# Attention and mixture-of-experts kernel: each head of a pair on its own 64 rows of the array for scores, transposed scores and halved mask matmuls

## The reference, cut to what matters

```python
def attention(X, enc, causal_mask, padding_mask, Wq, bq, Wk, bk, Wv, bv, Wo, bo):
    # 8 batches of 256 rows; 32 query heads of width 16; 8 key/value heads, each shared by 4 query heads
    q = (X @ Wq.T + bq).reshape(b, LQ, G, HPG, HD).transpose(0, 2, 3, 1, 4)
    k = (enc @ Wk.T + bk).reshape(b, LKV, G, HD).transpose(0, 2, 1, 3)
    v = (enc @ Wv.T + bv).reshape(b, LKV, G, HD).transpose(0, 2, 1, 3)
    scores = jnp.einsum('bgrqd,bgkd->bgrqk', q, k) / jnp.sqrt(HD)
    scores = jnp.where(causal_mask, -inf, scores)
    scores = jnp.where(padding_mask, -inf, scores)
    w = softmax(scores)
    out = jnp.einsum('bgrqk,bgkd->bgrqd', w, v)
    return out.transpose(...).reshape(b, LQ, HID) @ Wo.T + bo
x = x + tanh(g_xattn) * attention(layernorm(x), ctx, ...)
x = x + tanh(g_ffn) * experts(layernorm(x))      # 2 shared experts, 8 routed experts, top 2
```

## Time and profile before

| | us |
|---|---|
| median of 3 runs (1140.6 to 1146.6) | 1146.4 |
| span of the profiled execution | 1141.4 |
| PE busy / weight loads busy | 970.7 / 734.0 |
| DVE / ACT / POOL busy | 547.2 / 377.5 / 414.4 |
| attention, up to the start of the experts' matmuls | 562 |
| mean granted PE clock | 0.933 |

### The profile page before, as it was taken

How to read it: one execution, slowest core, us unless ns; L and a number is a source line. 1 busy time by engine, 2 the same in 40 slices (tenths; PEclk the granted TensorE clock), 3 DMA queues, 4 the chain that set the end, 5 groups by cost and what they waited for, 6 DMA issues and landing times.

```text
span 1141.4 us, 19977 instructions
## 1 busy us (share of the span) xinstructions
PE 970.7 (85%) x5240; PEld 734.0 (64%) x5241; DVE 547.2 (48%) x1679; ACT 377.5 (33%) x676; POOL 414.4 (36%) x513
## 2 busy tenths in 40 slices
PE   1477999999999999796499998999699898889894
PEld 1454555555555554343399987898598787778893
DVE  5286657676667677522233356633133333333331
ACT  2112544454445454362122252222122332133320
POOL 8713323333333303025100022053435665456542
PEclk9776999999999999997699997899899999999998
DMA  4333231414141323301451331143245544653442
GB/s 175 83 87 93 62 83 44 138 44 138 43 137 43 101 60 84 119 19 55 163 199 37 115 115 39 46 70 69 67 135 137 147 99 101 151 137 62 74 83 37
DMA packets 44943, 105.31 MB, mean 92 GB/s; under 512 B 8169, under 2 KB 12873, under 8 KB 43289
## 3 DMA queue, kind: packets, MB, share of 16 engines
q1 hardware_dynamic: 33064, 82.27, 24.3%
...
...
## 4 chain that ended last, share of the span: by engine, by line
PE 49%; DMA 12%; issue 11%; POOL 8%; DVE 8%; ACT 4%; POOLq 2%; ACTq 1%; SPq 1%; DVEq 0%
PE score_bank L516 5%; PE front_bank L464 5%; PE y_bank L1188 5%; PE gate_bank L1188 5%; PE up_bank L1188 5%; PE pv_bank L552 5%; DMA out_dram<-y,add_idx 5%; PE prob_bank L536 4%; PE tail_bank L464 4%; PE prob_bank L539 4%; POOL w_lo L126 3%; DMA x_ring<-xn_buf,gather_idx 3%; POOL row_table L1112 2%; DVE score_bank L780 2%; DMA row_table<-row_now 2%
## 5 line engine op out<-in xcount | busy, mean ns | idle before, releaser
L780 DVE CUSTOM_DVE_ANT_0 score_bank<-score_bank,mask 128x256 f32<-128x256 f32 x512 | 204.6, 449 | 123.5 <-PE score_bank L516 122.4
L669 ACT ACTIVATE probs<-prob_bank 128x512 f32<-128x512 f32 x256 | 150.0, 598 | 212.0 <-PE prob_bank L539 210.3
L516 PE MATMUL score_bank<-k_stack,q_stack 128*128 128x512 f32 x256 | 135.5, 533 | 31.0 <-DVE w_raw L780 16.7
L536 PE MATMUL prob_bank<-q_stack,k_stack 128*128 128x512 f32 x256 | 109.8, 436 | 15.4 <-DMA q_stack<-w_lo 12.8
L126 POOL TENSOR_TENSOR w_lo<-w_raw,w_hi (+2 forms) x20 | 70.7, 3721 | 118.5 <-ACT w_hi L120 118.5
L516 PEld LDWEIGHTS score_bank<-k_stack,q_stack 128*128 128x128 f32 x256 | 52.3, 205 | 92.9 <-DVE w_raw L780 64.5
L1399 DVE TENSOR_TENSOR h<-up_bank,silu 128x352 f32<-128x352 f32 x71 | 37.2, 525 | 154.3 <-PE up_bank L1188 118.2
L1188 PE MATMUL gate_bank<-w_hi,xt_hi 128*128 (+2 forms) x284 | 101.3, 357 | 4.5 <-DVE xt_lo L1391 2.5
L1188 PE MATMUL up_bank<-w_hi,xt_hi 128*128 (+1 forms) x284 | 93.9, 330 | 11.2 <-POOL w_lo L126 11.2
L539 PE MATMUL prob_bank<-maskT,w_raw 128*128 128x512 bf16 x256 | 102.6, 401 | 0.0
L1319 ACT ACTIVATE xt_hi<-xt_bank 128x512 fp32r<-128x512 f32 x71 | 42.5, 598 | 181.0 <-PE xt_bank L1221 168.6
...
## 6 DMA issues: line engine op xcount, KB each, us to landing
...
```

The source lines that it names most:

```text
L516: pe.matmul(bank[:].rearrange("p a b -> p (a b)"), q_stack[m.parity][:, gp, r, c * P:(c + 1) * P], k_stack[m.parity][:, gp].rearrange("p a ...
L536: pe.matmul(bank, k_stack[n.parity][:, gp, g2, kc * P:(kc + 1) * P], q_stack[n.parity][:, gp, 2 * rp:2 * rp + 2, :].rearrange("p a b -> p ...
L669: act.activation(probs[:, v % 8, :], prob_bank[v % 2][:].rearrange("p a b -> p (a b)"), ACT.Exp, scale=HD ** -0.5).then_inc(exp_done, 1)
L780: last = dve.tensor_tensor_reduce(out=bank[:, g2, :], in0=bank[:, g2, :], in1=mask[m.parity][:, c, :], scale=1.0, scalar=-3e38, op0=ALU.ad ...
```

## The change

A pair's two heads get disjoint halves of the array's rows. Source row j of a pair now lands in rows 4j, 4j+1 and 4j+2 for the three pieces (`stacked`), and rows 4j+3 hold the aux rows, so that head 0's 16 source rows fill rows 0 to 63 and head 1's fill rows 64 to 127. `k_stack` loses its second, zero-padded copy; `parity`, `k_raw` and one of two `k_hi` and `k_lo` operations go. A unit is now one head with both halves of its 256 queries (before: both heads, one half). Units are issued in pairs, in even slots: 4 score matmuls of 64 rows and 256 columns fill both score banks; 2 transposed-score matmuls of 64 rows and 512 columns fill both prob banks; the mask matmul of each bank is cut in a lower and an upper 64-row half, one before and one after the score matmuls, with a wait on a new semaphore `half_masked` between them. The waits of a pair's both units stand before its first score matmul (`score_ready` for u and u+1). `PROB_LAG` goes from 3 to 4, each half of `stack` issues 14 DMAs instead of 13, and the maxima go out in 2 DMAs.

```diff
-AUX = 3 * PAIR
+HALF = P // 2
+PARTS_A_ROW = 4
+AUX = 3
...
-PROB_LAG = 3
-PV_LAG = PROB_LAG + 5
+PROB_LAG = 4
+PV_LAG = PROB_LAG + 4
...
-STACK_DMAS = 13
+STACK_DMAS = 14
...
+        def stacked(stack, piece):
+
+            return stack[piece:P:PARTS_A_ROW]
+
+        def aux_rows(stack, g2, first=0, n=2):
+
+            lo = HALF * g2 + AUX + PARTS_A_ROW * first
+            return stack[lo:lo + PARTS_A_ROW * (n - 1) + 1:PARTS_A_ROW]
...
-                    for part, (q, k) in enumerate([(q_hi, k_hi), (q_hi, k_lo), (q_lo, k_hi)]):
-                        dst = slice(PAIR * part, PAIR * (part + 1))
-                        copy_rows(sp, qs[dst, gp, :, :], q[src, :, :]).then_inc(stack_in[half], 16)
-                        copy_rows(sp, ks[dst, gp, :, :], k[src, :, :]).then_inc(stack_in[half], 16)
-                copy_rows(sp, qs[AUX:AUX + 4, GP // 2 * half:GP // 2 * (half + 1), :, :], zeros).then_inc(stack_in[half], 16)
+                    for piece, (q, k) in enumerate([(q_hi, k_hi), (q_hi, k_lo), (q_lo, k_hi)]):
+                        copy_rows(sp, stacked(qs, piece)[:, gp, :, :], q[src, :, :]).then_inc(stack_in[half], 16)
+                        copy_rows(sp, stacked(ks, piece)[:, gp, :], k[src, :]).then_inc(stack_in[half], 16)
+                for g2 in range(2):
+                    copy_rows(sp, aux_rows(qs, g2)[:, GP // 2 * half:GP // 2 * (half + 1)].rearrange("o g r s -> o (g r s)"),
+                              aux_rows(k_stack[0], g2, 2, 4).rearrange("o g s -> o (g s)")).then_inc(stack_in[half], 16)
...
-            def score_unit(m, u):
-                gp, r, c = u // (R * QC), u // QC % R, u % QC
+            def score_ready(m, u):
+
                 if u % (SCORE_UNITS // 2) == 0:
-
                     at_least(pe, stack_in[2 * u // SCORE_UNITS], 16 * STACK_DMAS * (m.index + 1))
-                bank = score_bank[(m.parity + u) % 2]
                 if u == 0:
                     at_least(pe, maxima_done, SCORE_UNITS * m.index)
                 elif u == 1:
                     at_least(pe, maxT_copied, m.index)
                 else:
                     at_least(pe, maxima_done, SCORE_UNITS * m.index + u - 1)
-                pe.matmul(bank[:].rearrange("p a b -> p (a b)"), q_stack[m.parity][:, gp, r, c * P:(c + 1) * P],
-                          k_stack[m.parity][:, gp].rearrange("p a b -> p (a b)"),
-                          start=True, stop=True).then_inc(scores_done, 1)
+
+            def score_half(m, u, c):
+                gp, r, g2 = u // (R * 2), u // 2 % R, u % 2
+                rows = slice(HALF * g2, HALF * (g2 + 1))
+                last = pe.matmul(score_bank[(m.parity + u) % 2][:, c, :],
+                                 q_stack[m.parity][rows, gp, r, c * P:(c + 1) * P], k_stack[m.parity][rows, gp, :],
+                                 start=True, stop=True)
+                if c == QC - 1:
+                    last.then_inc(scores_done, 1)
+
+            def score_pair(m, u):
+
+                for k in range(2):
+                    score_ready(m, u + k)
+                for c in range(QC):
+                    for k in range(2):
+                        score_half(m, u + k, c)
...
-            def prob_unit(n, v):
+            def prob_scores(n, v):
...
                 at_least(pe, exp_done, PROB_UNITS * n.index + v - 1)
...
+            low, high = slice(0, HALF), slice(HALF, P)
+
+            def unit_pairs(s, n, score, soft, pair):
+
+                u, v = 2 * pair, 2 * pair - PROB_LAG
+                score, soft = score and u < SCORE_UNITS, soft and 0 <= v < PROB_UNITS
+                if soft:
+                    for k in range(2):
+                        prob_scores(n, v + k)
+                if soft and score:
+                    prob_mask(n, v, low, False, half_masked)
+                    prob_mask(n, v + 1, high, False, half_masked)
+                if score:
+                    score_pair(s, u)
+                if soft and score:
+                    at_least(pe, half_masked, (PROB_UNITS - PROB_LAG) * n.index + v + 2)
+                    prob_mask(n, v, high, True)
+                    prob_mask(n, v + 1, low, True)
+                elif soft:
+                    for k in range(2):
+                        prob_mask(n, v + k, slice(0, P), True)
...
-                    if score and slot < SCORE_UNITS:
-                        score_unit(s, slot)
-                    if soft and 0 <= slot - PROB_LAG < PROB_UNITS:
-                        prob_unit(n, slot - PROB_LAG)
+                    if slot % 2 == 0:
+                        unit_pairs(s, n, score, soft, slot // 2)
```

70 lines of the change are left out of this document (35 added, 35 removed).

## The result

| | before | changed |
|---|---|---|
| median, us | 1145.06 (4 runs) | 1174.63 (1164.39 to 1184.58, 4 runs) |
| ratio, 95% interval | | 1.0234 (1.0178 to 1.029) |
| span of the profiled execution | 1141.4 | 1182.8 |
| PE / DVE / ACT busy | 970.7 / 547.2 / 377.5 | 976.8 / 541.6 / 364.6 |
| the experts' first matmul | 562.6 | 595.4 |

The kernel became slower, by about the predicted time (1176). The profiled execution is the longest of the four (1184.58), 1.7% above the shortest, and is left out of the ratio; 8.6 of its extra 41.4 lie behind the start of the experts' matmuls, in code that the change doesn't touch: there PE's half-clock spells come and go from run to run. What the change did is read up to that start: 595.4 - 562.6 = 32.8 more, where 32.5 were forecast.

A forecast was written before the change was run, and what follows sets the result against it. PE and DVE were taken to alternate, with paired handshakes deciding. Iteration terms of 14.5 + 3 + 4.5 + 6.5 + 4 made +32.5 on the profiled 1141.4, so 1174, stated as 1176; 8-in-10 range 1152 to 1205.

The forecast's parts named there:

- The overlap: On PE, two 64-row halves run fully at the same time: four steps cost 0.95 a pair instead of 1.4, gaining 0.46.
- The rival with weight loads in series: Handshakes bind and score weight loads run one after another: 0.19 a pair, 21 more in all, 1197; chance 0.12.
- p4 to p6: Pairs of slots 8 to 13, with query blocks, a projection and the key/value block; PE-bound, forecast 0.7 shorter, 17.3 together.
- The handshakes: Deciding term: PE waits for both units of the last pair, losing overlap with DVE and ACT; +2.9 a full iteration.
- The ACT loop: A pair's second transposed-score matmul needs both previous exponentials, these the second mask halves behind the scores: 2.49 a cycle.
- The DVE loop: PE starts a pair's scores only after DVE finished both previous units: 0.05 + 0.41 + 1.46 + 0.14 = 2.06, plus extras.
- 0.5 for `tail_hi` between the exponentials: In the pair of slots 24 and 25, this ACT work adds 0.5, making the pair 3.0.
- The sign that DVE would wait 0.4 to 0.5 for scores in every light pair: Expected profile evidence in the eleven pairs without much other PE work: DVE waits 0.4 to 0.5 for scores.
- Over the iterations: Sum over attention: 14.5 (n = 1 to 5) + 3 + 4.5 + 6.5 (n = -1) + 4 (clock) = +32.5.
- The clock: Sparsely used PE drops to half clock in p1 and p2: 0.6 for each of seven iterations, +4.
- "Second maxima DMA: 0": The added maxima DMA lands before p2, where the first unit now stands, so it costs 0.
- The change of tiling: On PE, about 0.09 a switch; 6 new switches in p4 to p6 and p13, 0.5 in all; hidden in light pairs.

The follow-up runs named there:

- b1: The kernel before, full-row matmuls kept, with units issued in pairs and both whole masks behind the scores: 1178.72 us, ratio 1.0347.
- a3: The changed kernel's 64-row layout, with units issued one by one in the order and with the waits of before, whole masks: 1148.41 us, ratio 1.0101.
- the other profile: Second profile of the same changed kernel, from measuring it again: span 1170.2, experts from 590.1; that measurement gave 1173.98 us, ratio 1.0314.
- a4: The changed kernel plus extra matmuls, results never read, where PE stands idle in an iteration's first four pairs: 1167.11 us, ratio 1.0268.
- c1: The changed kernel with aux rows moved so that one DMA for the maxima serves both halves instead of two: 1172.06 us, ratio 1.0277.
- a6: a5 with transposed scores and whole masks issued in pairs in the iteration without scores: 1148.94 us, ratio 1.0101.
- a7: a6 with aux rows moved so that one DMA for the maxima serves both halves instead of two: 1140.57 us, ratio 1.0013.
- a5: a3's single units, with the paired form only in slots 10, 12, 14 and the last score pair (28): 1145.5 us, ratio 1.0057.

## Why the prediction was right

**The overlap** was taken as full, and the array gives it: in 100 of 128 score pairs the two heads' first matmuls start within 10 ns of each other. The transposed scores get less of it: only in 52 of 128 pairs do the two start within 20 ns, in most of the others the second starts 0.2 to 0.7 later, 0.49 most often, since it waits for an exponential of its own. The rival with weight loads in series falls too: its 21 more are not in the time, and p4 to p6 come out at 17.4 at full clock, where 0.19 more a pair would make it 17.9. The steps are longer than 0.24 all the same: the ten matmuls of p5 took 1.14, which is the forecast's 0.95 with its 0.1 for `half_masked` and its 0.09 for a switch.

**The handshakes** were the deciding term, and b1 and a3 show both halves of it: the pairing without the row halves costs 60.40 an iteration, the row halves without the pairing 55.94. By pieces (medians over n = 1 to 5 of the times from a pair's first score matmul to the next pair's):

| | forecast | measured |
|---|---|---|
| p0, p1, p2, p3 | 2.2, 3.0, 2.8, 2.5 | 2.41, 2.90, 2.93, 2.84 |
| p4 to p6 | 17.3 | 18.8, of it p4 6.64; 17.4 at full clock |
| p7, p8, p9 | 3.2, 3.0, 3.1 | 2.92, 3.06, 2.99 |
| p10, p11, p12 | 2.85, 2.5, 3.0 | 2.63, 2.45, 2.59 |
| p13, p14, p15 and end | 4.7, 2.5, 6.8 | 4.30, 2.42, 7.0 |

The ACT loop of 2.49 is seen bare in p11 (2.45) and p14 (2.42). The DVE loop shows in n = -1, where its pairs are 2.6 at half clock (forecast 2.4). Its first term was short: DVE starts 0.50 or more after a pair's first score matmul, not 0.41. (The forecast's own 2.4 less 1.8 is 0.6 a pair, not 0.65.) The largest single miss among the light pairs was p12, where 0.5 for `tail_hi` between the exponentials was too much. The sign that DVE would wait 0.4 to 0.5 for scores in every light pair did not come: in n = 3 its longest such wait runs from 0.1 (p11) to 1.3 (p7).

**Over the iterations** the sum is right with errors of both signs: n = -1 +7.8 (forecast 6.5), n = 0 +2.1 (3.6 with its clock share), n = 1 to 5 +20.6 (17.5 with theirs), n = 6 up to the first transposed score of n = 7 +5.4 (5.1), n = 7 and 8 -0.2 (0). One term was missing: the first scores start at 50.5 instead of 53.4, so -2.9 before any of it; the forecast gave the shorter front nothing.

**The clock** was the mis-sized term: 0.6 an iteration was forecast, and over n = 1 to 5 p4 alone is on the mean 1.4 over its full-clock 5.2 (1.2 in the other profile). So the sum came out to 0.3 by errors that cancel: the clock and n = -1 too low, against the 2.9 of the earlier start and light pairs p10 to p13 that were forecast too long. Half-clock spells begin in p2 or p3, as forecast for p1 to p3, but run on into p4, where PE is the bound and each us at 0.50 costs half of it: p4 is 0.4 to 2.6 over that 5.2. a4 showed that p4's excess is the clock, and also that filling the idle time does not remove the loss.

**"Second maxima DMA: 0"** was right for this kernel (c1: 0.07 an iteration) for a reason not given: the paired p0 is bound by its banks. With single units the same DMA costs 0.5 (a6 to a7), in ACT's issue time and not at the unit that reads the rows.

**The change of tiling** was priced at 0.09 from a full-array mask to column tiles. (The row it was held against, 260.30, is no full-array matmul: its tile is 128*64. The step of 0.24 between two full ones, 223.57 to 223.81, gives about the same price.) That is the cheap direction. From 64 rows to 128 it is 0.20, and the change avoids it between masks and scores, which are 64-row forms both (314.68 to 314.88, 0.20). From transposed scores to masks it is 0.34 (243.61 to 243.95) with no change of tiling, and no run shows why. Kernels with single units pay the 0.20.

What stays open: why the iteration without scores took 46.20 and 43.80 with single units. The switches explain some, but those kernels also ran its beginning at half clock for longer, 17 us in a3 and 12 in a5 against 5. a3 and a5 issue the same matmuls there, and 5.3 more of half clock go with 2.3 more of time; at that rate the clock makes about 3 of a5's 7.2, and 4 are left for the switches. That is an estimate, well under the 0.29 for each of 32 units, or 9, that the rows of a3 would give, and no run separates the two.
